# VectorE makes a pair's target indicators with two comparisons of two scalars each, in place of one operation with three operands

## The chip, the cores and the metric

One core of one Trainium2 chip runs the whole program. The metric is the time of one execution on the device, in microseconds (us). The engines are PE (TensorE), DVE (VectorE), ACT (ScalarE), POOL (GpSimd) and SP (SyncE, which only issues DMAs here). Each has a queue of its own that also executes register arithmetic, branches, assertions and waits; the profile writes that queue's own instructions as DVEq, PEq and so on, and does not count them as busy time.

## The reference, cut to what matters

A graph of 3125 nodes with 128 features and 100,000 edges (`src`, `dst`, sorted by `dst`; the density of targets falls as one over the square root of the node number, so low nodes have by far the most edges) goes through four layers, each of the form `x = layernorm(x + layer(x, edges))`: an edge MLP with batch norms, a two-way GCN, four rounds of a symmetric GCN, and an attention over edges. The last three need only, for each pair (target, source), how many edges run between them:

```
C[t, s] = number of edges e with dst[e] == t and src[e] == s        # 3200 x 3200 after padding
```

The change is in the stage that makes C, the count stage. A tile is 128 consecutive edges, one edge on each partition. For a window of 32 targets, the edges of two tiles (a pair of tiles, called a pair from here on) are turned into indicators, and TensorE multiplies them:

```
one_src[e, j] = (src_low[e] == j)                    # 800 columns, j = 0 .. 799
one_dst[e, r] = (row_c[e] + window_at[w] == r)       # 128 rows of the window,  row_c = 4*dst + src_high
counts[r, j] += sum over e of one_dst[e, r] * one_src[e, j]
```

A row r of a window stands for one of 32 targets and one of the four quarters of the sources; a row outside 0 .. 127 belongs to another window and matches nothing.

## The kernel before, in words

The program is written engine by engine, with semaphores between the engines and register loops whose limits are read from tables that the program makes itself. After a short preparation (to about 86 us) comes the count stage (86 to 774 us), then the statistics of the first layer, its two passes over the edges, and the later layers; the count stage is some 17% of the time.

In the count stage there are 100 windows and 468 pairs. VectorE's loop `count_four` handles four windows: it reads four words from `block_tab` (L1477), and for each window computes the first tile, the number of pairs and the number of pairs so far (L1480, L1481, L402). The first pair of a window is written out with `p = 0`; the others run in a register loop `Fori(1, length)` (L1485). So there are 100 first pairs and 368 pairs in loops. Early windows have up to some 40 pairs, late ones two or three. The function `one_hots(w, first, p, before)` makes one pair:

- It waits until the slot is free: the ring has 8 slots, `slot_free` is raised by TensorE at the end of each pair (L1834), and pair n needs pair n-8 to be done. For the first four windows (`w` a Python number, 82 pairs) this goes through `hold`, and it also waits on `one_ready` until the previous pair of its own has been completed. In the other 96 windows (386 pairs) it waits for the slot only.
- Two `tensor_scalar` (L1465), one for each tile, compare the 800 columns of `iota_sub` with that tile's `src_low`. All addresses (the slot of the ring, the column of the tile) come from registers.
- One operation with three operands (L1467) makes the 2 x 128 target indicators of both tiles, and raises `one_ready`.

TensorE waits for `one_ready`, does four matmuls of 400 or 401 columns for each pair (L1834), and once for each window some more: it moves the low part of the counts (L1854), sums source degrees (L1845) and closes the window (L1879). ScalarE takes the finished window out of PSUM (L994 to L996, L1008), and its DMAs store it. GpSimd issues the first layer's gathers (L841) in the same time; they are paced by `one_ready` up to round 13, and by `window_done` (thresholds up to window 92) up to round 16. The last window's counts go through L1008 and L1015, a maximum over them (L1494) closes the stage, and the next stage loads the counts back (from 777 us).

Of the kernel before, what the change touches and what calls it, by code (L numbers as in the profile page):

```python
# [21 lines left out]
P = 128  # L22
# [46 lines left out]
def side_at(side):  # L69
    return slice(SIDES[side][0] * P, SIDES[side][1] * P)  # L70
# [31 lines left out]
def gnn(nc, ins, out):  # L102
    f32, bf16, f16, i32 = mybir.dt.float32, mybir.dt.bfloat16, mybir.dt.float16, mybir.dt.int32
    ALU = mybir.AluOpType
    ACT = mybir.ActivationFunctionType
    AX = mybir.AxisListType
    ds = bass.ds
# [22 lines left out]
    with ctx:  # L130
        def sem(name):
            return ctx.enter_context(nc.semaphore(name))


        at = [-(-nc.sbuf_base // 64) * 64]
        size = {f32: 4, i32: 4, bf16: 2, f16: 2}

        def sb(name, shape, dt):
            n = size[dt]
            for s in shape[1:]:  # L140
                n *= s
            t = nc.alloc_sbuf_tensor_at(name, shape, dt, offset=at[0])
            at[0] += -(-n // 64) * 64
            assert at[0] <= nc.sbuf_usable_end, (name, at[0])
            return t
# [23 lines left out]
        iota_row = sb("iota_row", [P, P], f16)  # L169
# [3 lines left out]
        window_at = sb("window_at", [P, NWIN], f32)  # L173
# [7 lines left out]
        row_c = sb("row_c", [P, NT + 1], f32)  # L181
# [72 lines left out]
        one_dst = sb("one_dst", [P, PAIRS, 2, P], bf16)  # L254
# [88 lines left out]
        def bank(j, n=BANK):  # L343
            return psum[:, j * BANK:j * BANK + n]
# [19 lines left out]
        S = {n: sem(n) for n in names}  # L364
# [20 lines left out]
        def hold(name, eng, s, n):  # L385

            eng.wait_ge(s, n)
            eng.sem_inc(held[name], 1)
# [925 lines left out]
        def _(dve):  # L1314
            v = nc.vector
# [62 lines left out]
            for b in range(NB):  # L1378
                dve.wait_ge(S["ab_high"], b + 1)
                o = (b % 4) * BANK  # L1380
                v.scalar_tensor_tensor(a_parts[:, b, 1, :], psum[:, o:o + P], ab_up[:, 0:1].bitcast(f32),
                                       a_parts[:, b, 0, :], ALU.mult, ALU.subtract)
                last = v.scalar_tensor_tensor(b_parts[:, 1, b * P:(b + 1) * P], psum[:, o + P:o + 2 * P],
                                              ab_up[:, 0:1].bitcast(f32), b_parts[:, 0, b * P:(b + 1) * P],
                                              ALU.mult, ALU.subtract)
# [69 lines left out]
            def one_hots(w, first, p, before):  # L1455
                slot = (before + p) & (PAIRS - 1)
                at = nc.s_assert_within(dve.snap(first + p * 2), 0, NT - 1,
                                        skip_runtime_bounds_check_because="the limits end at the tile behind the last one")
                if isinstance(w, int):
                    hold("dve", dve, S["slot_free"], before + p + 1)  # L1460
                    dve.wait_ge(S["one_ready"], before + p)
                else:
                    dve.wait_ge(S["slot_free"], before + p + 1)
                for t in range(2):
                    v.tensor_scalar(one_src[:, ds(slot, 1), t, 0:SUB].rearrange("p o n -> p (o n)"), iota_sub[:, :],  # L1465
                                    src_low[:, ds(at + t, 1)], None, ALU.is_equal)
                v.scalar_tensor_tensor(one_dst[:, ds(slot, 1), :, :].rearrange("p o t n -> p (o t) n"),  # L1467
                                       row_c[:, ds(at, 2)].rearrange("p (t o) -> p t o", o=1).broadcast_to([P, 2, P]),
                                       window_at[:, ds(w, 1)],
                                       iota_row[:, :].rearrange("p (o n) -> p o n", o=1).broadcast_to([P, 2, P]),  # L1470
                                       ALU.add, ALU.is_equal).then_inc(S["one_ready"], 1)

            total_dve = dve.alloc_register("pairs_made")
            dve.reg_mov(total_dve, PAIR0)
# [1 line left out]
            def count_four(i):  # L1476
                words = nc.values_load_multi_w_load_instructions(  # L1477
                    block_tab[0:1, 2, ds(4 * i, 4)], engines=[dve.engine], min_val=0, max_val=NPAIR * 1024 + NT)[1]
                for q in range(4):
                    first = nc.s_assert_within(dve.snap(words[q] & 1023), 0, NT - 4)  # L1480
                    length = nc.s_assert_within(dve.snap(words[q] >> 10), 2, NPAIR)  # L1481
                    before = pairs_before(dve, total_dve)
                    w = 4 * i + q
                    one_hots(w, first, 0, before)
                    with dve.Fori(1, length) as p:  # L1485
                        one_hots(w, first, p, before)
                    dve.reg_add(total_dve, total_dve, length)
# [194 lines left out]
            for k in range(GNN_LAYERS):  # L1682
                for side in range(2):
                    at = side_at(side)
# [27 lines left out]
            for b in range(NB):  # L1712
                dve.wait_ge(S["node_psum"], (1 + GNN_LAYERS) * NB + b + 1)
                last = v.tensor_tensor(vaug[:, b, :, 0:HD], bank(b % 4, P).rearrange("p (h d) -> p h d", h=H),
                                       bv_bc[:, :].rearrange("p (h d) -> p h d", h=H), ALU.add)
# [10 lines left out]
            for quad in range(QUADS):  # L1726
# [43 lines left out]
                with dve.Fori(0, NC) as j:  # L1770
                    for k in range(NB):
                        w = k // SC
# [552 lines left out]
```

## Time and profile before

| what | us |
|---|---|
| median of 3 runs | 4011.37 (4000.53 to 4015.42) |
| profiled execution, its own time | 4002.94 |
| span of the profiled execution | 4001.3 |
| DVE busy over the span | 2746.1 (69%) |
| PE busy over the span | 3332.1 (83%) |
| count stage, first comparison to last | 86.3 to 759.7 |
| closing maximum of the stage (L1494) | starts at 773.74 |
| mean granted clock of TensorE | 0.951 of full speed |

Busy shares are averages over stages with different limits, so they do not say what a stage is worth. What matters for this change is what happens between 86 and 774 us: which engine or queue runs without a pause there, and how much time one pair takes on it. A merged line of the timeline, such as an operation "x2" of 0.77 us, covers two instructions that overlap in the engine's pipeline; the distance between the starts of successive lines is what a steady engine needs.

### The profile page before, as it was taken

What the parts mean: (1) busy time and instruction counts of PE and PEld (TensorE: products, weight loads), DVE (VectorE), ACT (ScalarE), POOL (GpSimd) and SP (SyncE); (2) the same over time, 40 slices, a digit from 0 to 9 for tenths busy, and PEclk for the clock granted to TensorE, in tenths of its full rate; (3) what the DMA queues carried; (4) which work ended last, traced back from release to release, by engine and by line L of the source; (5) the groups of instructions that cost most, each with busy time, mean ns of one, the idle gap of its engine ahead of it and who ended that gap; (6) DMA issues with size and microseconds to landing.
All of it is one profiled execution on the core that took longest, in us unless ns stands there. A gap on an engine that the chain in (4) does not pass through costs nothing. (4 is left out here: it accounts for less than half of the span.)

```text
span 4001.3 us, 82488 instructions
## 1 busy us (share of the span) xinstructions
PE 3332.1 (83%) x20226; PEld 1639.8 (41%) x20227; DVE 2746.1 (69%) x3688; ACT 1589.2 (40%) x2188; POOL 970.8 (24%) x1056
## 2 busy tenths in 40 slices
PE   3577787778999688879989984999899989979995
PEld 2233333334445377776455552333222233332223
DVE  5788877535666466651132226999799999989995
ACT  2034567502222265541021112221588832218883
POOL 2777765666666322210000001000100000000000
PEclk8999999989999899989999996999899999989997
DMA  2345667787777587876647745111253331113343
GB/s 73 104 147 197 227 232 258 280 300 245 253 250 243 201 259 228 233 214 216 229 154 252 258 158 148 60 55 41 83 147 118 107 102 57 57 41 115 114 129 69
DMA packets 359816, 666.09 MB, mean 166 GB/s; under 512 B 134695, under 2 KB 221661, under 8 KB 358695
## 3 DMA queue, kind: packets, MB, share of 16 engines
q1 hardware_dynamic: 236288, 361.30, 28.7%
q10 hardware_dynamic: 98346, 252.14, 18.1%
q0 software_dynamic: 25088, 51.43, 5.0%
q8 instruction: 54, 0.88, 0.1%
q14 instruction: 40, 0.33, 0.0%
HBM read 431.81 MB, written 208.20 MB: 160 GB/s over the span
## 5 line engine op out<-in xcount | busy, mean ns | idle before, releaser
L1778 DVE SCALAR_TENSOR_TENSOR pw<-ex,c_full 128x1564 f32<-128x1564 f32 x400 | 680.9, 1784 | 35.2 <-ACT ex L1293 30.3
L1293 ACT ACTIVATE ex<-psum 128x782 f32<-128x782 f32 x800 | 609.8, 826 | 77.8 <-PE psum L2215 59.9
L1740 DVE CUSTOM_DVE_ANT_0 masked<-psum,masks 128x1784 bf16<-128x1784 f32 x320 | 552.2, 1785 | 64.8 <-ACT masks L1266 43.9
L841 POOL DMA_INDIRECT gat<-a_table,gidx x480 | 513.1, 1069 | 190.1 <-issue 113.5
L1834 PE MATMUL psum<-one_src,one_dst 128*128 x1872 | 384.7, 341 | 182.9 <-DVE one_dst L1467 148.9
L1465 DVE TENSOR_SCALAR one_src<-iota_sub,src_low 128x800 f16 x936 | 367.3, 434 | 148.1 <-PE psum L1834 65.6
L2224 PE MATMUL psum<-pw,vaug 128*32 128x391 f32 x3200 | 348.8, 508 | 30.0 <-DVE pw L1778 9.6
L1834 PEld LDWEIGHTS psum<-one_src,one_dst 128*128 x1872 | 174.3, 98 | 375.0 <-issue 294.3
L1266 ACT ACTIVATE masks<-masks,far 128x3128 bf16<-128x3128 bf16 x40 | 115.5, 2900 | 423.2 <-DMA masks<-ct_parts 423.2
L1098 ACT ACTIVATE r<-psum,vec 128x1024 f32<-128x1024 f32 x98 | 118.0, 1204 | 378.1 <-PE psum L1975 333.6
L2031 PE MATMUL psum<-w2s,r_in 128*128 128x128 f32 x1568 | 205.7, 286 | 25.8 <-issue 13.5
L2180 PE MATMUL psum<-qp,kp 96*128 96x446 bf16 (+1 forms) x700 | 173.0, 365 | 61.1 <-DVE mx L1740 31.3
L1467 DVE SCALAR_TENSOR_TENSOR one_dst<-row_c,window_at,iota_row 128x256 f16 x468 | 222.6, 476 | 0.0
L1612 DVE SCALAR_TENSOR_TENSOR u<-psum,u 128x1024 f16<-128x1024 f32 x98 | 119.9, 1224 | 146.4 <-ACT u L1149 146.1
L841 POOL DMA_INDIRECT a_direct<-a_table,src_i x192 | 183.8, 957 | 123.3 <-DMA a_direct<-a_table,src_i 51.3
L2031 PEld LDWEIGHTS psum<-w2s,r_in 128*128 128x128 f32 x1568 | 188.5, 197 | 39.9 <-issue 31.8
L1576 DVE CAST dst_bc<-psum 128x1024 f16<-128x1024 f32 x98 | 120.0, 1225 | 123.3 <-PE psum L1975 118.2
L2185 PE MATMUL psum<-qp,kp 96*128 96x448 bf16 x800 | 189.3, 360 | 0.0
L1982 PE MATMUL psum<-r,W2T 128*128 128x512 f32 x392 | 186.9, 599 | 0.0
L2044 PE MATMUL psum<-u,ohd 128*128 128x128 f16 x1952 | 144.9, 227 | 50.1 <-DVE ohd L1624 27.9
L2215 PE MATMUL psum<-kp,qp 99*128 (+1 forms) x800 | 173.1, 337 | 13.6 <-ACTq L1275 7.9
L926 POOL TENSOR_TENSOR y<-y,visit_sum 128x128 f32 x122 | 94.4, 774 | 356.9 <-ACT visit_sum L1164 356.9
(353 smaller groups left out, 4893.2 us busy)
## 6 DMA issues: line engine op xcount, KB each, us to landing
c_full<-c_whole SPq DMA_DIRECT2D x80, 977.5 KB, 5.1
r_edges<-r ACTq DMA_DIRECT2D x98, 512.0 KB, 4.7
r_in<-r_edges ACTq DMA_DIRECT2D x98, 512.0 KB, 3.8
c_ring<-ct_parts SPq DMA_DIRECT2D x100, 480.0 KB, 4.3
c_whole<-c_sum ACTq DMA_DIRECT2D x100, 400.0 KB
a_edges<-gat SPq DMA_DIRECT2D x148, 256.0 KB
a_in<-a_edges ACTq DMA_DIRECT2D x74, 512.0 KB, 4.6
c_ring<-ct_parts SPq DMA_DIRECT2D x100, 320.0 KB, 3.6
```

The costliest lines, as they stand in the source:

```text
L841: g.indirect_dma_start(to, None, a_table, bass.IndirectOffsetOnAxis(ap=rows, axis=0)).then_inc(landed, 16)
L1293: a.activation(ex[:, step_slot(n // 2), (n % 2) * 2 * CW:(n % 2 + 1) * 2 * CW].rearrange("p (h t) -> p h t", h=2), psum[:, o:o + 2 * BANK] ...
L1465: v.tensor_scalar(one_src[:, ds(slot, 1), t, 0:SUB].rearrange("p o n -> p (o n)"), iota_sub[:, :], src_low[:, ds(at + t, 1)], None, ALU.is ...
L1467: v.scalar_tensor_tensor(one_dst[:, ds(slot, 1), :, :].rearrange("p o t n -> p (o t) n"), row_c[:, ds(at, 2)].rearrange("p (t o) -> p t o" ...
L1740: v.tensor_tensor_reduce(out=masked[:, n % 2, 0:count * width].rearrange("p (c t) -> p c t", c=count), in0=psum[:, first * BANK:(first + c ...
L1778: v.scalar_tensor_tensor(pw[:, step_slot(k), :].rearrange("p (h t) -> p h t", h=HQ), ex[:, step_slot(k), :].rearrange("p (h t) -> p h t", ...
L1834: last = t.matmul(bank(2 * k + half, n), one_dst[:, ds(slot, 1), s, :].rearrange("p o n -> p (o n)"), one_src[:, ds(slot, 1), s, half * HA ...
L1982: last = t.matmul(bank(4 + 2 * s + half), W["W2T"][:, :], r1[:, s, half * GE:(half + 1) * GE], start=True, stop=True)
L2031: last = t.matmul(psum[:, s * UE + k * P:s * UE + (k + 1) * P], r1_in[:, s, k * P:(k + 1) * P], w2s[:, :], start=False, stop=True, skip_gr ...
L2185: t.matmul(bank(7, 448), kp[0:KQK, n // 2, 0:P], query(quad, n // 2)[0:KQK, 0:448], start=True, stop=True)
L2215: last = t.matmul(bank(2 * (n % 3) + e, CW), query(quad, hh)[0:KQK + 3, s0:s0 + P], kp[0:KQK + 3, hh, ds(j * CW, CW)], start=True, stop=True)
L2224: last = t.matmul(psum[hh * HW:(hh + 1) * HW, 6 * BANK:6 * BANK + CW], vaug[:, k, quad * HQ + hh, :], pw[:, step_slot(k), hh * CW:(hh + 1) ...
```

## The change

Only the target indicators of `one_hots` change. The three-operand operation over both tiles goes; in its place each tile gets a `tensor_scalar` of its own over the 128 columns of `iota_row`, which subtracts the window's offset and compares with that tile's `row_c` (`iota_row - window_at[w] == row_c`). The semaphore is raised by the second one. The values are whole numbers below 2^24, so the indicators are the same.

```
-                v.scalar_tensor_tensor(one_dst[:, ds(slot, 1), :, :].rearrange("p o t n -> p (o t) n"),
-                                       row_c[:, ds(at, 2)].rearrange("p (t o) -> p t o", o=1).broadcast_to([P, 2, P]),
-                                       window_at[:, ds(w, 1)],
-                                       iota_row[:, :].rearrange("p (o n) -> p o n", o=1).broadcast_to([P, 2, P]),
-                                       ALU.add, ALU.is_equal).then_inc(S["one_ready"], 1)
+                for t in range(2):
+                    last = v.tensor_scalar(one_dst[:, ds(slot, 1), t, :].rearrange("p o n -> p (o n)"), iota_row[:, :],
+                                           window_at[:, ds(w, 1)], row_c[:, ds(at + t, 1)], ALU.subtract, ALU.is_equal)
+                last.then_inc(S["one_ready"], 1)
```

## Rows read from the trace of the kernel before

**Rows 1.** Page, part 5: busy us, mean ns of one, idle before.
```profile
L1834 PE MATMUL psum<-one_src,one_dst 128*128 x1872 | 384.7, 341 | 182.9 <-DVE one_dst L1467 148.9
L1465 DVE TENSOR_SCALAR one_src<-iota_sub,src_low 128x800 f16 x936 | 367.3, 434 | 148.1 <-PE psum L1834 65.6
L1467 DVE SCALAR_TENSOR_TENSOR one_dst<-row_c,window_at,iota_row 128x256 f16 x468 | 222.6, 476 | 0.0
```

**Rows 2.** Waits of DVE, 222 to 766 us: total us, times, longest.
```profile
DVE one_src L1465 <- PE psum L1834: 64.3, 55, 3.3
DVE one_src L1465 <- issue: 44.9, 44, 2.9
```

**Rows 3.** Windows with L1834's instructions alone: us, PE busy (x matmuls).
```profile
754.50:768.00 13.50, 6.64 (x32) 2.78 (x32) 1.00 0.80 282
509.10:768.00 258.90, 141.29 (x696) 63.43 (x694) 0.95 0.72 253
```

**Rows 4.** Windows with L1467's instructions alone: us, DVE busy (x operations).
```profile
754.50:768.00 13.50, 1.88 (x4) 1.00 0.80 282
509.10:768.00 258.90, 80.41 (x169) 0.95 0.72 253
```

**Rows 5.** Timeline of DVE, first four windows: start us, us, instruction.
```profile
101.28 0.77 DVE L1465 TENSOR_SCALAR one_src<-iota_sub,src_low 128x800 f16 x2 [0.42 <-DVE one_dst L1467]
101.96 0.48 DVE L1467 SCALAR_TENSOR_TENSOR one_dst<-row_c,window_at,iota_row 128x256 f16 x1
102.86 0.77 DVE L1465 TENSOR_SCALAR one_src<-iota_sub,src_low 128x800 f16 x2 [0.42 <-DVE one_dst L1467]
```

**Rows 6.** Timeline of DVE, a window turn and a loop later on.
```profile
504.17 0.80 DVE L1465 TENSOR_SCALAR one_src<-iota_sub,src_low 128x800 f16 x2 [2.37 <-issue]
505.29 0.75 DVE L1465 TENSOR_SCALAR one_src<-iota_sub,src_low 128x800 f16 x2
505.96 0.47 DVE L1467 SCALAR_TENSOR_TENSOR one_dst<-row_c,window_at,iota_row 128x256 f16 x1
506.36 0.75 DVE L1465 TENSOR_SCALAR one_src<-iota_sub,src_low 128x800 f16 x2
509.19 0.78 DVE L1465 TENSOR_SCALAR one_src<-iota_sub,src_low 128x800 f16 x2 [0.62 <-PE psum L1834]
```

**Rows 7.** Lines L1465 (first row: from 101 us), L1467, L1485: queue's instructions, ns min/median/max.
```profile
L1465 DVEq FUSED_REGOPS  x4: 93/139/179, 101.0 to 102.9; - x4
...
L1465 DVEq ALU_OP  x836: 40/45/50, 86.0 to 758.3; - x168
L1467 DVEq FUSED_REGOPS  x468: 76/76/93, 86.5 to 758.6; - x156
L1485 DVEq FUSED_REGOPS  x368: 58/58/73, 86.7 to 757.9; - x184
L1485 DVEq ALU_OP  x368: 40/40/45, 88.3 to 758.7; - x184
L1485 DVEq COMPARE_BRANCH  x368: 43/56/80, 88.3 to 758.8; - x184
```

**Rows 8.** Lines L1481, L402: the same, work at the turn of a window.
```profile
L1481 DVEq FUSED_REGOPS  x99: 237/264/271, 152.9 to 756.4; - x99
L402 DVEq FUSED_REGOPS  x99: 227/234/234, 153.2 to 756.7; - x99
```

**Rows 9.** DVE groups by shape, before the stage: busy us, mean ns of one.
```profile
L1381 DVE SCALAR_TENSOR_TENSOR a_parts<-psum,ab_up,a_parts 128x128 f16<-128x128 f32 x25 | 8.6, 345 | 1.8 <-ACT b_parts L965 1.7
```

**Rows 10.** Timeline of DVE and PE at the stage's end.
```profile
759.19 0.47 DVE L1467 SCALAR_TENSOR_TENSOR one_dst<-row_c,window_at,iota_row 128x256 f16 x1
773.74 0.26 DVE L1494 TENSOR_REDUCE over<-over 128x1 f32<-128x100 f32 x1 [14.07 <-ACT over_out L1015]
766.05 0.85 PE L1834 MATMUL psum<-one_src,one_dst 128*128 x4
781.23 16.34 PE L1908 MATMUL psum<-c_ring,b_parts 128*128 128x512 bf16 x70 [4.69 <-DMA c_ring<-c_parts]
```

## The prediction, before the changed kernel had run

> **What bounds the kernel now.** The change touches only the count stage (86 to 774 us), so I read that stage alone. The page's groups come first [rows 1]. DVE is busy 367 + 223 = 590 us of some 674 us there, PE 385 us with L1834, and PE's largest idle cause is that it waits for the target indicators, 148.9 us. That points to VectorE. But the same rows say that DVE was idle 148.1 us, 65.6 us of it put down to PE, which would mean a full ring and some slack. The waits of the later part put 64.3 us on PE and 44.9 us on "issue" [rows 2]. Which of the two is true is the question on which the forecast hangs.
>
> I checked it by counting pairs. At 509.19 DVE starts a pair after an idle of 0.62 us put down to PE [rows 6]. From there to the end it makes 169 pairs [rows 4], so this is pair number 468 - 169 = 299 (from zero), and it needs pair 291 to be done. PE has 696 / 4 = 174 pairs left to start [rows 3], so it has started 294: the slot had been free for some time. At 754.5 DVE has 4 pairs left and PE 8 [rows 3, 4]: pair 464 needs 456, and 460 had been started. So the ring was not full, and both idle causes are the same thing: the queue of VectorE doing register work. At the turn of a window two fused register operations alone take 264 + 234 ns [rows 8], and every fourth window the idle is 2.37 us [rows 6].
>
> Inside a loop the queue is as close. A pair of a loop costs the queue's own instructions: wait 45, address 179 (the longer of the two of a pair), tile address 45, second address 93, target address 76, loop 40 + 56 + 58: together 592 ns in 8 instructions [rows 7]. The measured period is 505.29 to 506.36, 1.07 us [rows 6]. The remaining 0.48 us over 8 instructions is 60 ns of gap behind each, in which engine instructions are handed over. The engine itself needs 2 x 0.335 for the source comparisons (505.29 to 505.96) and 0.40 for the target operation (505.96 to 506.36) [rows 6], which is also 1.07 us. Within a loop engine and queue are therefore level; at window turns the queue is alone. From 222 us on, time is the sum of what the queue does.
>
> The first four windows (82 pairs, 86 to 222 us) are different. Each pair waits for the completion of the one before: DVE idles 0.42 us behind each [rows 5], and the period is 101.28 to 102.86 = 1.58 us. There the engine's latency sets the time, and the queue has 1.58 - 1.07 = 0.51 us to spare in every pair.
>
> **The change part by part.** *Engine time of a pair.* Removed: one operation over 256 columns, 0.40 us from start to start. Added: two comparisons over 128 columns. The trace has no such operation, so I size it. 256 columns against 128 of the old kind are 476 against 345 ns [rows 1, 9], 1.02 ns a column; so of 0.40 us, 0.26 are columns and 0.14 are fixed. The source comparison takes 0.335 us for 800 columns; less the same fixed 0.14, that is 0.25 ns a column, four times the rate, with a scalar from memory and 16-bit data, as in the new comparison. So a new one takes 0.14 + 0.03 = 0.17 us, two 0.34, and a pair gains 0.06 us. The other bound is that the second scalar loses the fast rate: 0.14 + 0.13 = 0.27 each, 0.54 for two, a loss of 0.14. I take the gain, since L1465 is the nearest row.
>
> The Trainium skill's page "VectorE: DVE Perf Modes" (section on the TRN2 errata) counts 58 cycles plus columns divided by the rate at 0.96 GHz. By it the new pair of comparisons would take about 190 ns against 330, a gain of 0.14 us (an estimate); the trace's start-to-start distances show a larger fixed part. The same page ("Rules for kernel authors") speaks against this change: keep down the number of operations. What that number costs here is not a fixed part of the engine but the next step.
>
> *Queue time of a pair.* Removed: one target address, 76 + 60 ns. Added: two, and in a loop also the sum `at + 1`, for the second tile. The source comparisons show that pattern: the 836 plain ALU operations of L1465 are 468 waits plus 368, one for each pair of a loop and none for a first pair [rows 7]. So the second comparison costs 93 + 60 = 153 ns in a first pair, and 45 + 60 more, 258 ns, in a loop. The lower bound is that the sum is shared with the source side: 76 + 60 = 136 to 153 ns everywhere. The upper bound is a second address computation as long as the first source one (179 + 60 + 105, some 340 ns), or the window's address computed twice. I take 153 and 258, since the code repeats the source side's form exactly.
>
> *Sum, later windows (386 pairs).* 96 first pairs x 0.153 = 14.7 us; 386 - 96 = 290 loop pairs x 0.258 = 74.8 us; together 89.5 us. All of it is on the path, because the queue has no pause to hide it in. The engine's 0.06 us gain is worth nothing here: the new period is 1.07 + 0.26 = 1.33 us against an engine need of 1.01.
>
> *First four windows (82 pairs).* The added 0.26 us of queue work fit in the spare 0.51 us, partly while the long comparisons run. The shorter engine chain counts: 82 x 0.06 = 4.9 us gained (at the other bound, 82 x 0.14 = 11.5 us lost).
>
> *What is late at the end.* PE starts its last pair at about 766.2 while DVE finished it at 759.7 [rows 10]: PE lags 6.5 us behind, from bursts in which it was the slower one. When DVE is slower, PE will wait at DVE's heels, as it did at the start, and this lag goes: about 6 us back. What then follows (the last low parts, L1015, the maximum at 773.74, the load of `c_ring`, PE at 781.23 [rows 10]) waits only for the end of the stage and moves as a whole. GpSimd's gathers are paced by the same pairs and windows, so they shift along with it, and I give them nothing.
>
> Sum: + 89.5 - 4.9 - 6 = + 78.6 us. Against the profiled execution's own time, 4002.9, that is 4081.5; against the median, 4011.4, it is 4090. The profiled run is 8 us under the median, well within the three runs. I name 4085, between the two.
>
> **The rivals.** (1) *Shared address work.* The sum `at + 1` is not repeated: 386 x 0.153 = 59, less 10.9, + 48 us, 4051 to 4059. For it: it is the same value. Against: L1465 shows plain ALU work that exists only for the second tile. (2) *Fast rate lost.* + 89.5 + 11.5 - 6 = + 95 us, 4098 to 4106. The later windows don't notice it, since the engine's 2 x 0.335 + 0.54 = 1.21 us stays under 1.33. For it: no row has two scalars from memory. Against: L1465 keeps the fast rate with one. (3) *PE hides much of it.* If the 64.3 us put down to PE [rows 2] are true waits for a slot, they swallow that much: 89.5 - 64 - 5 = + 20 us, 4023 to 4032. Against it stands the count of pairs at two of those very places. (4) *The engine decides, and the change wins.* If the queue works ahead during the long comparisons, so that its period hides behind the engine's, every pair gets 0.06 us shorter: 468 x 0.06 = 28 us less, 3975 to 3983. It decides if the queue's share of a loop pair after the change, 1.33 us by my working, is really under 1.01 us, which needs gaps of under 30 ns instead of 60. For it: inside a loop the period equals the engine's sum to 0.01 us. Against: 592 ns of bare queue work plus some 140 to 200 more are already 0.75 to 0.8 without a single gap, and the turns of windows show that gaps exist.
>
> **How the numbers follow.** A measurement of this kernel can tell about 0.5%, 20 us, from no change. Forecast 0.66, rival 1 0.13, rival 2 0.10, rival 3 0.06, rival 4 0.05. The first three are slower by over 20 us; rival 3 lies on that bound and is split. Slower 0.91, within 0.5% 0.04, faster 0.05. The range reaches from rival 1 at the lower baseline (4048) to the forecast with a longer address computation (0.31 instead of 0.26 in a loop, 15 us more) and a lost fast rate at the higher baseline (4122): 4047 to 4122.
>
> **What would show it.** Right: the last comparison of the stage near 838 us in place of 759.7; the idle of DVE before L1465 put down to PE or "issue" hardly changed, but new idle ahead of the second target comparison or of the next L1465 within loops; a loop period near 1.33 us; queue instructions at the new line with as many plain ALU operations as loop pairs (368), or more; PE's wait for `one_dst` up from 148.9 us by some 80; a first-windows period near 1.52 us; all stages after the count as long as before. Wrong: a loop period of 1.2 us (shared address), of 1.07 or less (engine decides), a new comparison of over 330 ns (fast rate lost), or later stages that shrink because the gathers had more time.

## The result and the profile after

The changed kernel takes 4076.36 us (median of 4 runs, 4074.78 to 4080.99) against 4005.95 us of the kernel before in the same series: ratio 1.0186, 95% interval 1.0166 to 1.0207, or 70 us slower by the medians (75 by the ratio). The profiled executions are 4002.94 and 4074.78 us. The time was forecast 9 us too long and lies in the range. Three terms of the sum were off, though, by 28, 15 and 12 us, and made up for each other: that the time came out so near is luck.

The page of the changed kernel, part 5 (line, engine, operation | busy us, mean ns of one | idle before, releaser), answers to [rows 1]:

```profile
L1833 PE MATMUL psum<-one_src,one_dst 128*128 x1872 | 412.6, 357 | 219.7 <-DVE one_dst L1468 201.0
L1465 DVE TENSOR_SCALAR one_src<-iota_sub,src_low 128x800 f16 x936 | 375.4, 443 | 175.9 <-issue 80.2
L1468 DVE TENSOR_SCALAR one_dst<-iota_row,window_at,row_c 128x128 f16 x936 | 253.2, 313 | 0.0
```

PE waits 201.0 us for the target indicators, 52 more than before. DVE is busier by 39 us and also idler by 28 us; more idle in a longer stage points to something in front of the engine. (The two DVE groups overlap in the engine's pipeline, and their times can't be added: all DVE work between 86 and 760 us before is 529 us by the view of that window, not the 590 that the prediction names.) The queue's own instructions, as in [rows 7] (ns min/median/max, first and last start):

```profile
L1468 DVEq FUSED_REGOPS  x936: 69/69/93, 85.3 to 840.2; - x188
L1468 DVE TENSOR_SCALAR one_dst<-iota_row,window_at,row_c x936: 295/308/430, 85.8 to 840.8; 128x128 f16 x188
L1468 DVEq ALU_OP  x72: 45/45/45, 245.3 to 839.0; - x72
```

There are two address computations for each pair where there was one, and no plain ALU operation in the loops: the 72 are one for each of three windows in four, as many as L1467 had before. The new comparison takes 308 ns.

The timeline of DVE (start us, us, instruction) shows the first four windows, to be held against [rows 5]:

```profile
100.66 0.77 DVE L1465 TENSOR_SCALAR one_src<-iota_sub,src_low 128x800 f16 x2 [0.44 <-DVE one_dst L1468]
101.34 0.53 DVE L1468 TENSOR_SCALAR one_dst<-iota_row,window_at,row_c 128x128 f16 x2
102.31 1.00 DVE L1465 TENSOR_SCALAR one_src<-iota_sub,src_low 128x800 f16 x2 [0.44 <-DVE one_dst L1468]
```

101.34 to the end of the second comparison is 0.53 us where the old operation took 0.48, and 100.66 to 102.31 is 1.65 us where it was 1.58. The engine's chain is longer, not shorter.

In the fifth window, the first that does not wait for its own previous pair, the distances in the changed kernel are 235.42 to 236.93 to 238.45, 1.52 us for each pair of the loop:

```profile
235.42 0.77 DVE L1465 TENSOR_SCALAR one_src<-iota_sub,src_low 128x800 f16 x2 [0.31 <-issue]
236.10 0.64 DVE L1468 TENSOR_SCALAR one_dst<-iota_row,window_at,row_c 128x128 f16 x2
236.93 0.77 DVE L1465 TENSOR_SCALAR one_src<-iota_sub,src_low 128x800 f16 x2 [0.19 <-issue]
237.62 0.53 DVE L1468 TENSOR_SCALAR one_dst<-iota_row,window_at,row_c 128x128 f16 x2
238.45 0.77 DVE L1465 TENSOR_SCALAR one_src<-iota_sub,src_low 128x800 f16 x2 [0.30 <-issue]
```

Before, the same window ran at 1.07 us, without idle:

```profile
225.74 0.76 DVE L1465 TENSOR_SCALAR one_src<-iota_sub,src_low 128x800 f16 x2
226.42 0.48 DVE L1467 SCALAR_TENSOR_TENSOR one_dst<-row_c,window_at,iota_row 128x256 f16 x1
226.81 0.76 DVE L1465 TENSOR_SCALAR one_src<-iota_sub,src_low 128x800 f16 x2
```

In the changed kernel the other three inner loops run at medians of 1.29, 1.27 and 1.27 us a pair, and the first at 1.52. So this one loop is slower than the others, which the working did not foresee; E8 and E9 below are about it. Even 1.27 us is not what the engine needs: in the loop at 519 us the distance between two lines of L1468 is once 518.92 to 520.04, 1.12 us, and then 1.24.

```profile
518.92 0.53 DVE L1468 TENSOR_SCALAR one_dst<-iota_row,window_at,row_c 128x128 f16 x2
519.37 0.76 DVE L1465 TENSOR_SCALAR one_src<-iota_sub,src_low 128x800 f16 x2
520.04 0.53 DVE L1468 TENSOR_SCALAR one_dst<-iota_row,window_at,row_c 128x128 f16 x2
520.57 0.79 DVE L1465 TENSOR_SCALAR one_src<-iota_sub,src_low 128x800 f16 x2
521.28 0.52 DVE L1468 TENSOR_SCALAR one_dst<-iota_row,window_at,row_c 128x128 f16 x2
```

Where the 1.27 us come from can be read in the trace from the starts of the queue's nine instructions of a pair. From 260.635 to 261.901 us they lie 123, 180, 151, 151, 72, 190, 108, 78 and 213 ns apart, together 1.27 us, and in the next pair each step is the same to 1 ns. One of the two steps of 151 ns is the added address (69 ns of work and the way to the next instruction).

The turn of a window at the same place, and the waits of DVE from 225 to 845 us, which answer to [rows 2] (total us, times, longest):

```profile
257.00 0.77 DVE L1465 TENSOR_SCALAR one_src<-iota_sub,src_low 128x800 f16 x2 [0.67 <-PE psum L1833]
258.20 0.81 DVE L1465 TENSOR_SCALAR one_src<-iota_sub,src_low 128x800 f16 x2
259.47 0.77 DVE L1465 TENSOR_SCALAR one_src<-iota_sub,src_low 128x800 f16 x2
```
```profile
DVE one_src L1465 <- issue: 75.8, 85, 3.4
DVE one_src L1465 <- PE psum L1833: 55.6, 58, 2.8
```

The trace settles what the waits put down to PE are, if for each of them the end of TensorE's pair n-8 (ends are modelled there) is held against the start of the idle. Before, the slot had been free already in 49 of the 55 cases (median 2.1 us earlier), and at most 1.8 of the 64.3 us were true waits for it. In the changed kernel it had been free for 5.7 us or more in all 58. For the same reason TensorE's lower granted clock in the stage (0.91 after, 0.97 before, and 357 in place of 341 ns for a matmul) is no cause of the loss.

The end of the stage (DVE and PE), which answers to [rows 10]:

```profile
840.59 0.52 DVE L1468 TENSOR_SCALAR one_dst<-iota_row,window_at,row_c 128x128 f16 x2
849.83 0.26 DVE L1493 TENSOR_REDUCE over<-over 128x1 f32<-128x100 f32 x1 [8.71 <-ACT over_out L1015]
```
```profile
842.59 0.85 PE L1833 MATMUL psum<-one_src,one_dst 128*128 x4
```

DVE's last target operation starts 81.4 us later (759.19 to 840.59), PE's last pair only 76.5 (766.05 to 842.59), the closing maximum 76.1 (773.74 to 849.83). PE's lag shrank by 5 us, close to the 6 that were forecast. The stage's end comes 76.1 us later and the profiled executions differ by 71.8, so the count stage accounts for all, and some 4 us come back in later stages.

For the comparisons that follow, two times are taken from each profiled execution's timeline: the *first four windows*, from the first comparison to the first comparison of the fifth window (82 pairs), and the *later windows*, from there to the start of the last pair (385 distances). The stage starts between 84.9 and 88.6 us. Behind the closing maximum the eleven profiled executions take 3221 to 3241 us, whatever the form of a pair, so a difference of some us in the totals says little about the stage.

| kernel | first four | later | median us | ratio to before (95%) |
|---|---|---|---|---|
| before | 137.3 | 534.9 | | |
| changed | 144.1 | 610.6 | 4076.36 | 1.0186 (1.0166 to 1.0207) |
| E1 two semaphore increments a pair, old form | 138.0 | 622.8 | 4090.56 | 1.0218 (1.0189 to 1.0247) |
| E2 old form over 344 columns | 144.7 | 535.7 | 4035.18 | 1.0079 (1.0051 to 1.0107) |
| E3 new form, one scalar | 134.4 | 593.3 | 4054.31 | 1.0122 (1.0093 to 1.0151) |
| E4 new form in the first four only | 144.9 | 544.9 | 4015.27 | 1.0032 (1.0019 to 1.0046) |
| E5 new form in the later ones only | 137.3 | 598.3 | 4063.35 | 1.0147 (1.0117 to 1.0176) |
| E6 old form, no wait for its own pair | 102.9 | 535.5 | 3973.14 | 0.9913 (0.9891 to 0.9935) |
| E7 new form, no wait for its own pair | 119.1 | 610.7 | 4053.86 | 1.0122 (1.0099 to 1.0145) |
| E8 changed, code shifted | 145.4 | 595.9 | 4066.90 | 1.0148 (1.0126 to 1.0171) |
| E9 before, code shifted | 138.5 | 543.5 | 4010.21 | 1.0012 (1.0001 to 1.0023) |

### The profile page after: what moved, and what is told of

It is laid out like the page before. It is cut to its first block and busy times, and to the rows that moved or that the text cites. A ratio compares the mean times of both kernels' runs of the same rounds, so it can differ in the third digit from the quotient of the medians.

```text
span 4073.1 us, 83424 instructions
## 1 busy us (share of the span) xinstructions
PE 3371.5 (83%) x20226; PEld 1643.5 (40%) x20227; DVE 2800.7 (69%) x4156; ACT 1590.1 (39%) x2188; POOL 925.0 (23%) x1056
## 5 line engine op out<-in xcount | busy, mean ns | idle before, releaser
L1739 DVE CUSTOM_DVE_ANT_0 masked<-psum,masks 128x1784 bf16<-128x1784 f32 x320 | 552.0, 1785 | 64.3 <-ACT masks L1266 44.2
L1833 PE MATMUL psum<-one_src,one_dst 128*128 x1872 | 412.6, 357 | 219.7 <-DVE one_dst L1468 201.0
L841 POOL DMA_INDIRECT gat<-a_table,gidx x480 | 477.9, 996 | 223.5 <-issue 123.1
L1465 DVE TENSOR_SCALAR one_src<-iota_sub,src_low 128x800 f16 x936 | 375.4, 443 | 175.9 <-issue 80.2
L1468 DVE TENSOR_SCALAR one_dst<-iota_row,window_at,row_c 128x128 f16 x936 | 253.2, 313 | 0.0
L2214 PE MATMUL psum<-kp,qp_next 99*128 (+1 forms) x600 | 169.2, 338 | 13.2 <-SPq L452 7.6
```

What stands on the lines that cost most here:

```text
L841: g.indirect_dma_start(to, None, a_table, bass.IndirectOffsetOnAxis(ap=rows, axis=0)).then_inc(landed, 16)
L1468: last = v.tensor_scalar(one_dst[:, ds(slot, 1), t, :].rearrange("p o n -> p (o n)"), iota_row[:, :], window_at[:, ds(w, 1)], row_c[:, ds( ...
L1739: v.tensor_tensor_reduce(out=masked[:, n % 2, 0:count * width].rearrange("p (c t) -> p c t", c=count), in0=psum[:, first * BANK:(first + c ...
L1833: last = t.matmul(bank(2 * k + half, n), one_dst[:, ds(slot, 1), s, :].rearrange("p o n -> p (o n)"), one_src[:, ds(slot, 1), s, half * HA ...
L2214: last = t.matmul(bank(2 * (n % 3) + e, CW), query(quad, hh)[0:KQK + 3, s0:s0 + P], kp[0:KQK + 3, hh, ds(j * CW, CW)], start=True, stop=True)
```

## The experiments

Theory Q: from the fifth window on, VectorE's queue is the time, and each instruction added to a pair costs its queue time in full; in the first four, the engine's chain is. Rival E came up with the result: the engine's own need of a pair had risen too (0.335 + 0.335 + 0.22 + 0.31 us, 1.20 in place of 1.07, from the starts in the loop at 519 us), and 468 x 0.13 = 61 us would explain most of the loss without any queue. That is an upper bound: at 519 us a pair took 1.12 us, 0.05 more than before.

**E1. Queue time alone.**

```
+                for k in range(2):
+                    dve.sem_inc(ticks[k], 1)
                 v.scalar_tensor_tensor(one_dst[...
```

> The kernel before, with two semaphore increments (on semaphores that nobody waits for) added to each pair ahead of the target operation. They cost VectorE's queue time and its engine none. Theory Q (from the fifth window on, the queue's own work is the time; in the first four the engine's chain is): each increment takes some 60 to 80 ns of queue, so 386 x 0.12 to 0.16 = 46 to 62 us in the later windows, nothing in the first four, less some 4 us of TensorE's lag: +42 to +58 us. Rival E (the time came from the engine, whose need of a pair rose from 1.07 to 1.20 us): the engine does the same as before, so 0 to +5 us.

Measured: later windows 534.9 to 622.8, + 87.9 us; the first four 137.3 to 138.0; in all + 86 us where 42 to 58 were expected. The engine's work is the same (L1470, 476 ns in the mean, 468 times), and still the loss is more than the whole change brought. Rival E is out as the only cause. The size was missed: the trace gives each increment 21 ns, and the distance to its neighbours in the queue comes on top.

```profile
L1469 DVEq EVENT_SEMAPHORE  x936: 21/21/21, 86.3 to 847.2; - x188
```

Here too the first inner loop was a slow one (below): 1.55 us in place of 1.31 over 51 distances, so some 12 of the 88 us belong to that; the rest is 76 / 770 = 99 ns for each increment, not 60 to 80. In E8, 16 increments in a row make the way from one pair to the next 1.8 us longer, 115 ns each.

**E2. Engine time alone.**

```
-        iota_row = sb("iota_row", [P, P], f16)
+        iota_row = sb("iota_row", [P, 172], f16)
-        one_dst = sb("one_dst", [P, PAIRS, 2, P], bf16)
+        one_dst = sb("one_dst", [P, PAIRS, 2, 172], bf16)
...
-                                       row_c[...].broadcast_to([P, 2, P]),
+                                       row_c[...].broadcast_to([P, 2, 172]),
```

> The kernel before, with the three-operand operation over 2 x 172 columns in place of 2 x 128; TensorE reads the first 128 as before. The queue has the same work; the engine has 88 columns more, at 1.02 ns each 0.09 us for each pair. Rival E: 468 x 0.09 = +42 us. Theory Q: 82 x 0.09 = +7 us in the first four windows, and in the later ones only what long loops lose, where the engine's 1.16 us passes the queue's 1.09: some 0 to 10 us. Together +7 to +17 us.

Measured in the stage: the first four windows + 7.4 us (0.09 x 82 to the tenth), the later ones + 0.8 us, although every pair keeps the engine 0.09 us longer there as well. In the loop at 504 us the engine now sets the distance (1.16 to 1.20 us), and the turn of the window gives it back. Over all later windows the distances within them grow by 31.6 us together, and those across the turns shrink by 30.7. So engine time is paid in the first four windows, and in the later ones this form gets it back, which fits a queue that runs ahead while the engine works and so is through with the turn sooner.

```profile
503.88 0.75 DVE L1465 TENSOR_SCALAR one_src<-iota_sub,src_low 128x800 f16 x2
504.56 0.56 DVE L1467 SCALAR_TENSOR_TENSOR one_dst<-row_c,window_at,iota_row 128x344 f16 x1
505.04 0.79 DVE L1465 TENSOR_SCALAR one_src<-iota_sub,src_low 128x800 f16 x2
```

The whole kernel lost more than the stage, 31 us by the medians and 26 by the profiled executions. Of the 26, 2 come before the stage, 8 in it, 2 between its last pair and the closing maximum, and 14 in later stages. About half of these 14 lie in the first edge pass (495.8 us against 489.2), which the edit touches only by moving every later tile in SBUF; but that pass takes 479 to 496 us in the eleven profiles, 494.7 in E6, which moves nothing. By its total alone this run would have spoken for rival E (42) as much as for Q (7 to 17). The cause of the 14 us stays open.

**E3. One scalar in place of two.**

```
-                                           window_at[:, ds(w, 1)], row_c[:, ds(at + t, 1)], ALU.subtract, ALU.is_equal)
+                                           row_c[:, ds(at + t, 1)], None, ALU.is_equal)
```

> The changed kernel, with target comparisons that have one scalar from memory (row_c) and no second one: the window's offset is left out, so the counts of all but the first window are zero; loops and instructions are as many. It tells what the second scalar costs, and whether the engine's part matters. Theory Q: the new comparison falls from 0.31 to about 0.25 us, the first four windows' period from 1.70 to about 1.57 us (82 x -0.13 = -10 us against the changed kernel), the later windows keep their loss but for a few ns of hand-over: against before about +58 to +64 us. Rival E: the engine's need falls to about 1.05 to 1.1 us, as before, so the whole loss goes: -5 to +10 us against before.

```profile
L1468 DVEq FUSED_REGOPS  x936: 69/69/76, 88.8 to 816.7; - x188
L1468 DVE TENSOR_SCALAR one_dst<-iota_row,row_c x936: 235/248/478, 89.3 to 817.2; 128x128 f16 x188
```

The kernel leaves out the window's offset, so its counts are wrong. The comparison takes 248 ns instead of 308: the second scalar from memory costs 60 ns. From start to start of two in a row it is 0.16 us with one scalar, where the prediction had sized 0.17, and 0.22 with two, between its 0.17 and the 0.27 of a lost fast rate. Whether the 60 ns are a fixed price or one of each column can't be told, as only 128 columns were run. The first four windows fall by 9.7 us against the changed kernel and are 2.9 us under before, which is the gain that the prediction had put there (4.9). The later windows keep 58.4 of the 75.7 us (the slow first inner loop is in both) though the engine's need is now under the old one: Q again, not E. By the medians it is + 50 us in all, nearer to Q's + 58 to + 64 than to E's - 5 to + 10, but outside both.

The later windows fell by 17.3 us, more than the "few ns of hand-over" expected, and here the engine counts after all. 9.7 us of it lie in the 96 distances from a window's first pair to its second: 257.00 to 258.20, 1.20 us, in the changed kernel above, and 250.07 to 251.14, 1.07, here.

```profile
250.07 0.80 DVE L1465 TENSOR_SCALAR one_src<-iota_sub,src_low 128x800 f16 x2 [0.84 <-PE psum L1833]
251.14 0.98 DVE L1465 TENSOR_SCALAR one_src<-iota_sub,src_low 128x800 f16 x2
252.38 0.77 DVE L1465 TENSOR_SCALAR one_src<-iota_sub,src_low 128x800 f16 x2
```

The difference, 0.12 us in the medians of three windows in four, is twice the 60 ns. Most of the rest, 6.9 us, lies in the loops (1.24 in place of 1.27 us): four of the queue's nine steps are 6 to 8 ns longer with two scalars. The missing address of the window (the 72 plain ALU operations) may have a part; no run separates it.

**E4 and E5. The new form in one part of the windows only.**

```
+                if isinstance(w, int):        # E4; E5 has "not isinstance(w, int)"
+                    for t in range(2):
+                        last = v.tensor_scalar(one_dst[...], iota_row[:, :], window_at[...], row_c[...], ALU.subtract, ALU.is_equal)
+                    last.then_inc(S["one_ready"], 1)
+                else:
                     v.scalar_tensor_tensor(one_dst[...
```

> The other half of e5: the new form only in the first four windows, the old one in all later ones. Theory Q: there the chain of a pair is the engine's, longer by about 0.08 us with the second scalar's price (1.17 to 1.25 us), so 82 x 0.08 to 0.1 = +7 to +8 us in those windows, the later ones as before (535 us), unless the code, which lies 16 instructions further on, puts the first inner loop over the border (then 8 to 9 us more there, of which TensorE's lag hides some 5). Together +7 to +12 us. Rival (my prediction's engine gain): -5 us.

> The new form only in the windows from the fifth on, the old one in the first four. Theory Q: the first four windows as before (137 us), the later ones as in the changed kernel: +60 to +68 us against before. Rival E: the loss is spread by pairs, 386 of 468: about +50 to +58 us, and then the first four windows would account for 10 to 15 us of the change.

E4: first four + 7.6 us, later + 10.0 without any change in their instructions, + 13 us in all by the ratio. E5: first four unchanged, later + 63.4, + 59 us in all, just under the 60 to 68 expected. So the first four windows carry a small loss and the later ones the rest. But E5's later windows are 12.3 us shorter than the changed kernel's with the same instructions. Both oddities are the same thing, and E8 and E9 test it.

**E8 and E9. The place of the code.** In the changed kernel the first of the four inner loops takes 1.52 us a pair. In E5, whose code lies 16 instructions earlier (the first four windows have the shorter old form), that loop takes 1.26. E8 shifts the changed kernel's loops by 16 instructions that run once, E9 the old kernel's by 15. These stand between the first four windows and the fifth, so 1.8 and 1.3 us of the column "first four" are theirs.

```
             count_four(0)
+            for _ in range(16):
+                dve.sem_inc(tick, 1)
             with dve.Fori(1, NWIN // 4) as i:
```

> The changed kernel, with 16 semaphore increments (nobody waits for them) once, ahead of the register loop over the later windows: no work in any pair, but the loops' code lies 16 instructions further on. In the changed kernel the first of the four inner loops takes 270 ns from its branch to the next instruction where the others take 135, and 150 against 50 before the next wait. Theory L (this is the place of the code, some border inside that loop): the shift takes it off, 75 passes x 0.24 = -15 to -18 us against the changed kernel, so +53 to +57 against before. Rival (the loop is slow for what it does): 0 to +2 us against the changed kernel, +70 to +73 against before.

> The kernel before with 15 such increments at the same place. Theory L: its first inner loop now lies over the border, so its gap behind the branch goes from 135 to about 270 ns, and it loses 10 to 18 us. Rival: 0 to +2 us.

E8, the timeline of DVE in the same loop: 234.79 to 236.06 to 237.32, 1.26 us and no idle.

```profile
234.79 0.77 DVE L1466 TENSOR_SCALAR one_src<-iota_sub,src_low 128x800 f16 x2
235.47 0.58 DVE L1469 TENSOR_SCALAR one_dst<-iota_row,window_at,row_c 128x128 f16 x2
236.06 0.76 DVE L1466 TENSOR_SCALAR one_src<-iota_sub,src_low 128x800 f16 x2
236.74 0.58 DVE L1469 TENSOR_SCALAR one_dst<-iota_row,window_at,row_c 128x128 f16 x2
237.32 0.77 DVE L1466 TENSOR_SCALAR one_src<-iota_sub,src_low 128x800 f16 x2
```

E9, the old form, which ran at 1.07 there: 226.40 to 227.98 is 1.58, then 1.33.

```profile
226.40 0.85 DVE L1466 TENSOR_SCALAR one_src<-iota_sub,src_low 128x800 f16 x2
227.17 0.47 DVE L1468 SCALAR_TENSOR_TENSOR one_dst<-row_c,window_at,iota_row 128x256 f16 x1
227.98 0.98 DVE L1466 TENSOR_SCALAR one_src<-iota_sub,src_low 128x800 f16 x2 [0.33 <-issue]
228.88 0.47 DVE L1468 SCALAR_TENSOR_TENSOR one_dst<-row_c,window_at,iota_row 128x256 f16 x1
229.31 0.77 DVE L1466 TENSOR_SCALAR one_src<-iota_sub,src_low 128x800 f16 x2
```

E8's later windows are 14.7 us shorter than the changed kernel's, E9's 8.6 us longer than before: the theory holds both ways. The other runs agree. In the kernel before, E2, E5 and E6, whose code ahead of the loops is no longer than before, the first inner loop is as fast as the others. In the changed kernel, E1, E3, E4, E7 and E9, where up to 16 instructions more stand there, it is slow, in either form; in E8, with 32 more, it is fast again. The extra time of a pass lies in two places of the queue: behind the branch, where the next instruction starts 319 ns later in place of 190, and behind that one, 208 in place of 108 (changed kernel, 236 us).

In the totals both fell short of what was expected. E8's closing maximum comes 12 us earlier than the changed kernel's, and by the medians it gives back 9 us (4076 to 4067) where 15 to 18 were expected. E9's last pair starts 10.3 us later than before, its maximum 6.6 (PE's lag hides the difference, which the expectation had left out), and it costs 3.6 us by the medians where 10 to 18 were expected. The Trainium skill ("Advanced Engine Details and Errata", ISA Cache) says that the cache of instructions has two lines of 256 instructions each. A border of such a line inside a loop would fit; the runs show that the place matters and not what lies there.

**E6 and E7. Without the wait for its own previous pair.** That wait stands only in the first four windows.

```
                     hold("dve", dve, S["slot_free"], before + p + 1)
-                    dve.wait_ge(S["one_ready"], before + p)
```

> The kernel before, in the first four windows without the wait for the completion of its own previous pair (the wait for the slot stays). The ring and the semaphores keep it safe. Theory Q: the period there falls from 1.60 us to what TensorE or the queue needs, 1.15 to 1.2 us: 82 x 0.4 = -33 us, perhaps -25 if GpSimd's gathers, which are paced by the pairs, come in the way. Rival (that wait is cheap because TensorE or the gathers set the pace): 0 to -8 us.

> The changed kernel without that wait. Theory Q: the queue decides in all windows then, with 1.25 to 1.3 us a pair: the first four fall from 144 to about 106 us, -35 us against the changed kernel, +33 to +40 against before. Rival (engine's chain decides there even without the wait): the period stays over 1.5 us, -10 us or less.

```profile
103.08 0.76 DVE L1464 TENSOR_SCALAR one_src<-iota_sub,src_low 128x800 f16 x2
103.76 0.48 DVE L1466 SCALAR_TENSOR_TENSOR one_dst<-row_c,window_at,iota_row 128x256 f16 x1
104.28 0.77 DVE L1464 TENSOR_SCALAR one_src<-iota_sub,src_low 128x800 f16 x2
```

E6: 1.20 us a pair (103.08 to 104.28), first four windows 34.4 us shorter, and all of it arrives at the end: 3973 us, 33 under the kernel before by the medians and faster than both kernels. E7, the same place with the new form:

```profile
103.56 0.77 DVE L1464 TENSOR_SCALAR one_src<-iota_sub,src_low 128x800 f16 x2 [0.18 <-issue]
104.97 0.77 DVE L1464 TENSOR_SCALAR one_src<-iota_sub,src_low 128x800 f16 x2 [0.19 <-issue]
```

It takes 1.40 us a pair where 1.25 to 1.3 were expected, and the first four windows are 25 us shorter, not 38. In all it is + 47 us against before by the medians, outside the 33 to 40. With the wait gone, the new form costs 16.2 us in those 82 pairs (102.9 to 119.1), 0.20 each; with it, 6.8. The spare time of the queue behind the wait had hidden the rest, as the prediction had said of those windows. The queue's price in a loop is thus the same in all windows once nothing hides it: 1.40 - 1.20 here, 1.27 - 1.07 later.

## Why the prediction was right, point by point

- *What bounds the stage.* Right in the main. The queue of VectorE from the fifth window on, the engine's chain before: E2 (engine time comes back in the later windows, is paid in the first four), E1 (queue time the other way round) and E7 show each half. One part was missed: from a window's first pair to its second, the engine's time counts in the later windows too (E3, 9.7 us). The idle put down to PE was the queue's, as the counting of pairs had said and the trace shows for 49 of 55 waits; rival 3 is out.
- *Queue time of a pair.* The step that was mis-sized most. Taken: 0.153 us in a first pair, 0.258 in a loop, 89.5 us in all. Without the code's place it is E8's 595.9 - 534.9 = 61.0 us, 0.158 for each pair, the engine's part included; E5 gives 63.4, 0.16. The term with the repeated sum `at + 1` was wrong: L1468 has no plain ALU operation in the loops. For this term it is rival 1 that came true (59 us), to which the prediction gave 0.13; its sign, no plain ALU work for each pair of a loop, was there, and the loop period, 1.27 us, lies between its 1.2 and the forecast's 1.33.
- *Code place.* Not foreseen: 610.6 - 595.9 = 14.7 us. It is a real part of this change's cost, but an accident of where the loop lies.
- *Engine time of a pair.* Wrong in sign. A gain of 0.06 us was taken; the comparison with one scalar came out as sized, and the second scalar costs 60 ns in each of the two (E3), which had been put at nothing. The first four windows lost 6.8 us (E4: 7.6) where 4.9 were to be gained, inside the bounds that stood there (- 4.9 to + 11.5). The old form's 1.02 ns a column was taken from an operation that reads 32-bit numbers from PSUM [rows 9], which is not the same kind; E2 bears the figure out all the same (476 to 565 ns for 88 columns more).
- *TensorE's lag.* Right: 4.9 us against 6.
- *Gathers and later stages.* Some 4 us came back behind the stage, nearly all in the first edge pass (489 to 484 us). The gathers had hardly run further ahead by the stage's end (427 in the stage against 424). It is no effect of the new form: E8 has the same form and takes 489 us there, E9 has the old one and takes 483.
- *The other signs.* The last pair's target comparison came at 840.6 us where 838 was forecast. The period in the first windows was 1.65 us and not 1.52. PE's wait for `one_dst` rose by 52 us and not by 80, and the idle put down to PE or "issue" did change, from 113.9 to 136.6 us.

The sum by what was measured: + 6.8 + 61.0 + 14.7 - 1.2 (an earlier start of the stage) - 4.9 = + 76.4 at the end of the stage, less 4.5 in later ones, + 71.9. The forecast of + 78.6 was nearer than its steps deserve: 28 us too much for the queue, 15 too little for the code's place and 12 for the engine. What bounds the stage was understood; the size was luck.

## What to carry to other kernels

Count instructions, not only engine time, wherever addresses come from registers: here one more instruction, 0.22 us of the engine from start to start, took 0.15 us of the queue, and a pair of a loop became 0.20 us longer although the engine needed only 0.05 more. A fast form that needs two instructions where one did lost because the queue was level with the engine. Idle that a profile puts down to another engine is checked by counting: how many items each side has left at that moment says whether the ring was full. And a loop of a few long register instructions should be measured at two places in the code before a difference of a few tenths of a per cent is believed.

## What the runs showed of the hardware

- A comparison of 128 16-bit columns takes 248 ns with one scalar from memory and 308 ns with two (E3, changed kernel); from start to start 0.16 and 0.22 us.
- A semaphore increment of VectorE's queue, 21 ns in the trace, costs 99 ns in the mean in a stretch that the queue bounds (E1), and 115 ns in a row of 16 (E8).
- The place of a register loop in the instruction stream changed its period from 1.27 to 1.52 us (new form, E8 and the changed kernel) and from 1.07 to 1.32 us (old form, before and E9; medians), for the same instructions, when moved by 15 or 16 instructions.
- Idle of VectorE that the profile puts down to TensorE was in 49 of 55 cases (before) and 58 of 58 (after) idle with the slot already free.
